# Grouped expert FFN in one kernel: its opening re-ordered (LoRA A and B first, folds, adds and transposes in another order, products in three sweeps)

## What is computed

```
w = weight[adapter_ids];  y = einsum('bsi,boi->bso', x, w)
h = einsum('bsd,nrd->nbsr', y, lora_A);  coef = (2 * lora_weights)[:, None, None]
out = x + einsum('bsd,od->bso', y, W) + bias + einsum('nbsr,nor->bso', h, lora_B * coef)
```

## Time and profile before

| | |
|---|---|
| median of three runs | 1523.1 us |
| profiled execution, its own time | 1520.31 us |
| span in that execution | 1518.6 us |
| PE busy | 1494.0 us, 98% |
| DVE, POOL, ACT busy | 783.4, 460.9, 393.5 us |
| mean granted TensorE clock | 0.996 |

### The profile page before, as it was taken

How to read it: one execution, slowest core, us unless ns; L and a number is a source line. 1 busy time by engine, 2 the same in 40 slices (tenths; PEclk the granted TensorE clock), 3 DMA queues, 4 the chain that set the end, 5 groups by cost and what they waited for, 6 DMA issues and landing times.

```text
span 1518.6 us, 29617 instructions
## 1 busy us (share of the span) xinstructions
PE 1494.0 (98%) x6354; PEld 1192.3 (79%) x6355; DVE 783.4 (52%) x1192; ACT 393.5 (26%) x493; POOL 460.9 (30%) x645
## 2 busy tenths in 40 slices
PE   6989999999999999999999999999999999999998
PEld 3768888888888888888888888888888888888887
DVE  6687666477787277388853333333333433333332
ACT  4244333344444234244431111111111101111010
POOL 4355334433434523525102112112122121221211
PEclk9999999999999999999999999999999999999999
DMA  8988667566787566569835555555455554555554
GB/s 203 327 242 233 162 179 207 164 185 185 201 226 199 167 183 163 178 193 233 211 115 156 144 139 141 136 140 145 132 139 147 140 145 132 141 145 136 141 142 97
DMA packets 172737, 257.90 MB, mean 170 GB/s; under 512 B 31648, under 2 KB 135584, under 8 KB 172704
## 3 DMA queue, kind: packets, MB, share of 16 engines
q1 hardware_dynamic: 130000, 139.14, 35.9%
q10 hardware_dynamic: 22384, 72.76, 16.3%
q0 software_dynamic: 20320, 45.65, 10.4%
HBM read 181.93 MB, written 75.50 MB: 170 GB/s over the span
## 4 chain that ended last, share of the span: by engine, by line
PE 93%; DMA 3%; DVE 2%; SPq 1%; issue 1%; ACT 0%; DVEq 0%; POOL 0%; ACTq 0%; POOLq 0%
PE ps L753 31%; PE ps L755 31%; PE ps L754 31%; DMA x_raw<-in_x_dram 1%; DMA b_raw<-in_L_ffn_lora_B_dram 1%; SPq L207 1%; DMA weff<-fold_sb 1%; DVE w_lo L596 1%; DMA base_sb<-in_L_ffn_W_dram 1%; DVE w_turn L539 0%; SPq L196 0%; SPq L214 0%; DVE fold_sb L655 0%; DVE x_lo L634 0%; DVE x_turn L627 0%
## 5 line engine op out<-in xcount | busy, mean ns | idle before, releaser
L753 PE MATMUL ps<-w_hi,x_hi 128*128 (+1 forms) x2096 | 828.9, 395 | 6.6 <-issue 3.7
L754 PE MATMUL ps<-w_lo,x_hi 128*128 (+1 forms) x2096 | 828.2, 395 | 0.0
L755 PE MATMUL ps<-w_hi,x_lo 128*128 (+1 forms) x2096 | 828.2, 395 | 0.0
L753 PEld LDWEIGHTS ps<-w_hi,x_hi 128*128 128x128 f32 x2096 | 393.5, 188 | 105.8 <-issue 4.8
L755 PEld LDWEIGHTS ps<-w_hi,x_lo 128*128 128x128 f32 x2096 | 393.5, 188 | 96.7
L754 PEld LDWEIGHTS ps<-w_lo,x_hi 128*128 128x128 f32 x2096 | 393.6, 188 | 96.3
L627 DVE STREAM_TRANSPOSE x_turn<-x_raw 128x256 f32<-128x256 f32 x544 | 193.7, 414 | 510.5 <-DMA x_raw<-y_scr 456.0
L207 POOL DMA_DIRECT2D x_raw<-in_x_dram x552 | 294.7, 534 | 399.9 <-DVE x_turn L627 262.2
L421 ACT ACTIVATE x_hi<-x_turn 128x512 fp32r<-128x512 f32 x272 | 167.2, 630 | 697.4 <-DVE x_turn L627 681.0
L396 POOL TENSOR_TENSOR stage<-stage,w_place 128x1024 f32<-128x1024 f32 x64 | 152.8, 2388 | 611.1 <-DMA stage<-in_x_dram 611.1
L634 DVE TENSOR_TENSOR x_lo<-x_turn,x_hi 128x512 fp32r<-128x512 f32 x272 | 180.5, 691 | 133.1 <-ACT x_hi L421 128.4
(11 more groups left out here) (69 smaller groups left out, 38.3 us busy)
## 6 DMA issues: line engine op xcount, KB each, us to landing
w_place<-in_L_cond_weight_dram SPq DMA_DIRECT2D x480, 128.0 KB, 4.2
y_scr<-stage ACTq DMA_DIRECT2D x72, 512.0 KB, 4.1
x_raw<-in_x_dram POOLq DMA_DIRECT2D x552, 64.0 KB, 3.6
x_raw<-y_scr SPq DMA_DIRECT2D x512, 64.0 KB, 2.4
stage<-in_x_dram SPq DMA_DIRECT2D x128, 256.0 KB, 3.7
out_dram<-stage ACTq DMA_DIRECT2D x126, 256.0 KB, 3.0
base_sb<-in_L_ffn_W_dram POOLq DMA_DIRECT2D x8, 512.0 KB, 11.2
weff<-fold_sb POOLq DMA_DIRECT2D x8, 512.0 KB, 11.2
```

The source lines that it names most:

```text
L753: mm(ps[b][:, cols], x_hi[b][:, t, :], hi, start=t == 0, stop=False)
L754: mm(ps[b][:, cols], x_hi[b][:, t, :], lo, start=False, stop=False)
L755: last = mm(ps[b][:, cols], x_lo[b][:, t, :], hi, start=False, stop=t == KT - 1)
```

## The change

The two halved loads of A and B become one load each: A directly behind the ids on SyncE's queue, B first on ScalarE's. Three of the four loads of the first expert's weights (before: two) are issued before the routing tables are there. VectorE transposes only chunk 0, not 0 and 1, before it writes the tables. Five folds instead of six go ahead of slot 0. W gets eight buffers (two of them `stage`) instead of six. VectorE adds six eighths before the x of slot 2 and two behind it, and prepares slot 4's x in the middle of the second expert instead of ahead of it. Slot 4's x is loaded by GpSimd behind the stores of weff instead of by SyncE, and GpSimd's loads for slots 6 and on wait for `w_turned` 14. ScalarE moves slot 0's result only when all adds are done. And `products`, which serves the whole program, runs x_hi w_hi over all eight t, then x_lo w_hi, then x_hi w_lo, each sweep waiting only for its own operands.

```
-    BASES = 6
+    BASES = 8
...
+        base_sb = base_sb[:4] + stage + base_sb[4:]
...
             sp.dma_start(ids_i[:, :], ids.rearrange("(s a) -> s a", a=1)).then_inc(ids_loaded, 16)
-            load_first(sp, 0, (0, 1), w0_loaded)
-            load_b(sp, 0)
-            load_a(sp, 0)
-            load_first(sp, 1, (0, 1), w0_loaded)
+            sp.dma_start(a_sb[:, :], lora_a.rearrange("n r d -> (n r) d")).then_inc(a_loaded, 16)
+            for c in range(LOADS - 1):
+                load_first(sp, c, (0, 1), w0_loaded)
             sp.wait_ge(tables, 1)
             for h in range(2):
                 load_sample(sp, 0, 0, h, first_loaded[0], (0, 1))
-            for c in range(2, LOADS):
-                load_first(sp, c, (0, 1), w0_loaded)
+            load_first(sp, 3, (0, 1), w0_loaded)
...
-            for h in range(2):
-                load_sample(sp, RING, 0, h, first_loaded[0])
...
+            load_first(pool, LOADS - 1, (2, 3), w0_rest)
...
             pool.wait_ge(b_turned, 1)
-            for f in range(4):
+            for f in range(6):
+                load_base(f)
+            pool.wait_ge(w_turned, 6)
+            for f in range(6, FOLDS):
                 load_base(f)
             for h in range(2):
                 load_sample(pool, 3, 3, h, first_rest[3])
-            pool.wait_ge(w_turned, 6)
-            for f in range(4, FOLDS):
-                load_base(f)
             for f in range(FOLDS):
                 pool.wait_ge(base_added, f + 1)
                 pool.dma_start(fold_rows(weff, f), fold_sb[:, f, :]).then_inc(weff_ready, 16)
+            for h in range(2):
+                load_sample(pool, RING, 0, h, first_rest[0])
             load_x(RING + 1, 1)
+
+            pool.wait_ge(w_turned, 2 * CHUNKS - 2)
             load_x(RING + 2, 2)
...
-            load_first(act, 0, (2, 3), w0_loaded)
-            load_b(act, 1)
-            load_a(act, 1)
-            load_first(act, 1, (2, 3), w0_loaded)
+            act.dma_start(b_raw[:, :, :, :].rearrange("p n f r -> p n (f r)"),
+                          lora_b.rearrange("n (p f) r -> p n (f r)", f=FOLDS)).then_inc(b_loaded, 16)
+            for c in range(LOADS - 1):
+                load_first(act, c, (2, 3), w0_loaded)
...
+            act.wait_ge(base_added, FOLDS)
             move_y(0, 0, 0)
             round_x(3, 3)
+
+            act.wait_ge(weff_ready, 16 * FOLDS)
+            round_w(1, 1, range(0, CHUNKS // 2))
             round_x(4, 0)
-
-            act.wait_ge(weff_ready, 16 * FOLDS)
-            round_w(1, 1)
+            round_w(1, 1, range(CHUNKS // 2, CHUNKS))
...
             turn_w(0, 0)
-            turn_w(0, 1)
             dve.wait_ge(listed, 1)
...
             tsc(rank_expert[:, :], ps[2][0:1, 0:EXPERTS + 1], float(EXPERTS), None, ALU.add).then_inc(tables, 1)
+            turn_w(0, 1)
...
+            for f in range(6):
+                add_base(f)
             prepare_first(2)
...
+            for f in range(6, FOLDS):
+                add_base(f)
             prepare_first(3)
+            prepare_w(1, 1, range(0, CHUNKS // 2))
             prepare_first(4)
-            prepare_w(1, 1)
+            prepare_w(1, 1, range(CHUNKS // 2, CHUNKS))
...
-            for f in range(6):
+            for f in range(5):
                 fold(f)
...
+                    pe.wait_ge(w_rounded, ready + (half + 1) * CHUNKS // 2)
+                    for t in range(KT):
+                        if half == 0 and t % (KT // 2) == 0:
+                            pe.wait_ge(x_rounded, n * 2 + (1 + t // (KT // 2)))
+                        mm(ps[b][:, cols], x_hi[b][:, t, :], hi[t], start=t == 0, stop=False)
+                    if half == 0:
+                        pe.wait_ge(x_ready, n * 2 + 2)
+                    for t in range(KT):
+                        mm(ps[b][:, cols], x_lo[b][:, t, :], hi[t], start=False, stop=False)
                     pe.wait_ge(w_ready, ready + (half + 1) * CHUNKS // 2)
-                    cols = slice(half * HALF, (half + 1) * HALF)
                     for t in range(KT):
-                        hi = w_hi[:, bass.ds(par, 1), t, cols].rearrange("p a m -> p (a m)")
-                        lo = w_lo[:, bass.ds(par, 1), t, cols].rearrange("p a m -> p (a m)")
-                        mm(ps[b][:, cols], x_hi[b][:, t, :], hi, start=t == 0, stop=False)
-                        mm(ps[b][:, cols], x_hi[b][:, t, :], lo, start=False, stop=False)
-                        last = mm(ps[b][:, cols], x_lo[b][:, t, :], hi, start=False, stop=t == KT - 1)
+                        last = mm(ps[b][:, cols], x_hi[b][:, t, :], lo[t], start=False, stop=t == KT - 1)
...
             def run_slot(slot, u):
                 used = entry(pe, slot_used, 2 * slot, 1)
-                pe.wait_ge(x_ready, 2 * slot + 2)
                 with pe.If(used > 0):
...
                 with pe.Else():
 
+                    pe.wait_ge(x_ready, 2 * slot + 2)
```

More of the change, by code:

```diff
@@ L161, in grouped_adaln_ffn_kernel @@
         w0_loaded = [sem(f"w0_loaded{c}") for c in range(LOADS)]
-        w0_rest = [sem(f"w0_rest{c}") for c in range(LOADS)]
+        w0_rest = {LOADS - 1: sem("w0_rest")}
         w_loaded = [sem(f"w_loaded{b}") for b in range(RAWS)]
@@ L215, in load_first @@
                               rows[:, :, q * SEG:(q + 1) * SEG]).then_inc(loaded[c], 16)
[L217 to L226, removed]
         @block.sync
@@ L461, in _ @@
             round_x(0, 0)
-            for f in range(3, 6):
+            for f in range(3, 5):
                 move_fold(f)
             round_w(0, 0, [4, 5, 6, 7])
-            for f in range(6, FOLDS):
+            for f in range(5, FOLDS):
                 move_fold(f)
@@ L526, in turn_w @@
                     raw = first_raw[load][:, part * P // BLK:(part + 1) * P // BLK, :]
-                    if part == 0 and load < 2:
+                    if part == 0 and load < LOADS - 1:
                         dve.wait_ge(w0_loaded[load], 16 * QUADS)
@@ L650, in _, with add_base @@
             prepare_first(1)
+            def add_base(f):
+                dve.wait_ge(fold_moved, f + 1)
+                dve.wait_ge(base_loaded[f], 16)
+                tt(fold_sb[:, f, :], fold_sb[:, f, :], base_sb[f][:, :], ALU.add).then_inc(base_added, 1)
+            for f in range(6):
+                add_base(f)
             prepare_first(2)
[L652 to L655, removed]
+            for f in range(6, FOLDS):
+                add_base(f)
             prepare_first(3)
+            prepare_w(1, 1, range(0, CHUNKS // 2))
             prepare_first(4)
-            prepare_w(1, 1)
+            prepare_w(1, 1, range(CHUNKS // 2, CHUNKS))
             for slot in range(1, RING):
@@ L739, in _, with products @@
             pe.wait_ge(b_scaled, 1)
-            pe.wait_ge(a_loaded, 32)
-            for f in range(6):
+            pe.wait_ge(a_loaded, 16)
+            for f in range(5):
                 fold(f)
-            def products(b, par, ready, halves=range(2), end=False):
+            def products(b, par, n, ready, halves=range(2), end=False):
                 for half in halves:
+                    cols = slice(half * HALF, (half + 1) * HALF)
+                    hi = [w_hi[:, bass.ds(par, 1), t, cols].rearrange("p a m -> p (a m)") for t in range(KT)]
+                    lo = [w_lo[:, bass.ds(par, 1), t, cols].rearrange("p a m -> p (a m)") for t in range(KT)]
+                    pe.wait_ge(w_rounded, ready + (half + 1) * CHUNKS // 2)
[7 more added lines that the diff above has]
+                        mm(ps[b][:, cols], x_lo[b][:, t, :], hi[t], start=False, stop=False)
                     pe.wait_ge(w_ready, ready + (half + 1) * CHUNKS // 2)
-                    cols = slice(half * HALF, (half + 1) * HALF)
                     for t in range(KT):
-                        hi = w_hi[:, bass.ds(par, 1), t, cols].rearrange("p a m -> p (a m)")
-                        lo = w_lo[:, bass.ds(par, 1), t, cols].rearrange("p a m -> p (a m)")
-                        mm(ps[b][:, cols], x_hi[b][:, t, :], hi, start=t == 0, stop=False)
-                        mm(ps[b][:, cols], x_hi[b][:, t, :], lo, start=False, stop=False)
-                        last = mm(ps[b][:, cols], x_lo[b][:, t, :], hi, start=False, stop=t == KT - 1)
+                        last = mm(ps[b][:, cols], x_hi[b][:, t, :], lo[t], start=False, stop=t == KT - 1)
                 if halves[-1] == 1:
@@ L759, in products @@
                     last.then_inc(end_half, 1)
-            pe.wait_ge(x_ready, 2)
             pe.wait_ge(fold_moved, 2)
-            products(0, 0, 0, [0])
-            for f in range(6, FOLDS):
+            products(0, 0, 0, 0, [0])
+            for f in range(5, FOLDS):
                 fold(f)
-            products(0, 0, 0, [1])
+            products(0, 0, 0, 0, [1])
             def run_slot(slot, u):
                 used = entry(pe, slot_used, 2 * slot, 1)
-                pe.wait_ge(x_ready, 2 * slot + 2)
```

(14 more changed lines are left out.)

20 lines of the change are left out of this document (8 added, 12 removed).

## The result

The changed kernel took 1511.75 us (median of 6 runs, 1507.98 to 1512.28) against 1521.97 (6 runs beside it): ratio 0.9926, interval 0.9913 to 0.9939, 10.2 us less. The profiled execution took 1507.98 us with a span of 1506.3.

A forecast was written before the change was run, and what follows sets the result against it. PE was taken to be bound, its only idle time around the opening, so E counts: 9.7 us from E, plus 2.0 for a spell gone, minus 1.6 for a new one, gives 10.1 off 1523.1, 1513.0 us; range 1509.0 to 1518.8.

The forecast's parts named there:

- What bounds, and the spacing: PE never waits behind the opening; from 104 us a matmul starts every 233.3 ns, and the sweeps leave that unchanged.
- E: Start of slot 6's products on PE, the later of two chains' ends: 89.5 us forecast, 99.18 before.
- the slower rival: The sweeps widen the matmul spacing, paid 6288 times; 5 ns would cost 31 us, giving 1544; chance 0.04.
- B's landing, 12.0: B, whole at the head of ScalarE's queue, lands at 12.0 us, within bounds 5.0 to 13.0.
- First weights at 15: Chunk 0 of the first weights, behind A and B, reaches VectorE at 15 us; it was 11.24 before.
- PE's own chain, 89.5: Folds, slot 0, slots 1 to 4 and slot 5's dummy on PE end at 89.5 us.
- The charge for a new spell at half clock before slot 0 (1.6): PE's new 1.8 us idleness ahead of slot 0 was charged 1.6 us for running at half clock afterwards.
- weff ready at 62: Second expert's weff: last store issued at 54.4, landing after 7.6 us, so ready at 62 instead of 73.35.
- From weff to slot 6: Second expert's chain from weff to slot 6's rounded x: 23.3 us plus 2.7 for slot 4's x, ending at 88.0.
- the rival's mechanism (second expert last): Second expert late: weff ready only at 67, E 93.0, PE idles 3.5 us, time 1518.5; chance 0.18.
- The spell behind slot 6 goes (2.0): PE's half-clock spell from 99.18 to 103.97 us, after the wait before slot 6, disappears: 2.0 us gained.
- Slot 4's x in the chain behind weff: Preparing slot 4's x inside the second expert adds 2.7 us, but that chain's 88.0 stays under PE's 89.5.

The follow-up runs named there:

- e3_hold_expert: Changed kernel with SyncE waiting for all eight adds before loading chunks 2 and on of the second expert; 1509.17 us.
- e10_x4_hold: Changed kernel with slot 4's x loaded and prepared early, and the second expert's chunks 2 and on held until all adds are done; 1506.21 us.
- e11_x4_six: Changed kernel with slot 4's x loaded and prepared early, and six folds instead of five ahead of slot 0; 1507.68 us.
- e1_halves: Changed kernel with A and B loaded as two halves again, behind load 0 of the weights; 1514.48 us.
- e8_x2_first: Changed kernel with slot 2's x prepared ahead of the six adds again; 1513.81 us.
- e9_six_buffers: Changed kernel with six buffers for W, the seventh and eighth loads waiting for adds behind slot 3's x; 1513.15 us.
- e6_six_folds: Changed kernel with six folds instead of five ahead of slot 0; 1510.72 us.
- after_again: The changed kernel timed and profiled once more, no edit; 1511.36 us.
- e7_x4_early: Changed kernel with slot 4's x loaded by SyncE behind slot 2's and prepared ahead of the second expert; 1507.16 us.
- e2_old_products: Changed kernel with products in their old order, three matmuls per t, waiting for x_lo and w_lo first; 1513.05 us.
- e5_sweeps_alone: Kernel before the change with only the products in three sweeps; 1520.75 us, ratio 0.9996.

## Why the prediction was right, and where its steps failed

The forecast took 10.1 us off the median, and 10.2 were measured. Step by step it was right in some and lucky in others.

- **What bounds, and the spacing**: right. All that changed lies ahead of E; the long stretch has 233.3 to 233.4 ns per matmul in every kernel, so the slower rival fell. Three of the kernels with an early E show 0.6 to 0.7 us of idle time in it (e3_hold_expert, e10_x4_hold, e11_x4_six), so there E is not quite all that counts.
- **B's landing, 12.0**: failed by 5.7 us; it landed at 6.3, near the low bound of 5.0. B and A, 1 MB together, were in at 6.3 and 6.6, both about 4 us after the first data, some 250 GB/s. The forecast had B share the engines from its first piece. In the trace 803 of the 1024 pieces on B's queue had been moved by 4.0 us, against 2 of A's 128, and only from 4.5 to 5.5 us did the queues go one for one, 77 pieces against 79. That second part fits the turn-taking the Trainium skill describes ("DMA: Bandwidth & Descriptors", "Queues, rings and completion order"). The head start, which the forecast lacked, brought B in; why A began so late, issued 0.5 us behind B, is open. The folds started 5.2 us before the 16.4 of the forecast. The forecast also said that an early B would hardly change the sum; e1_halves, with the whole old opening, is 3.1 us slower.
- **First weights at 15**: failed, 11.34. By then 2.6 MB had been moved, not 3, and the rate from 4 to 16 us was 313 GB/s, not 250. Slot 0 started at 23.17 for 27.3, so the title's part is worth more than the 1.0 us of the folds: 2.9 alone, 3.1 inside the change.
- **PE's own chain, 89.5**: it ended at 86.7 (88.95 less the idle 2.24). The charge for a new spell at half clock before slot 0 (1.6) was right for this profile: the next sweep starts 3.40 us after 23.17, where 8 x 0.2333 = 1.87 would do, 1.5 lost. In e8_x2_first, e9_six_buffers and e10_x4_hold that spell is absent.
- **weff ready at 62**: 62.2, by two errors that cancel. The last store was issued at 50.63, not 54.4, and landed after 11.55 us, not 7.6. The count by bytes gave the right number (18 MB at 312 GB/s; the trace has 18.5 MB at 318 from 4 us to 62.2): the DMA engines set this landing, not the last add.
- **From weff to slot 6**: right, 26.0 forecast; the first half of slot 6's x was rounded at 88.1, 25.9 later.
- **E, 89.5**: 88.95 and 90.67 in two profiles, but set by the second expert, which the forecast had 1.5 us under PE's chain. That is the rival's mechanism (second expert last) at the forecast's size, and PE was idle for 2.24 us where the forecast allowed 1. The chain that ended last goes through weff in both profiles, and in e6_six_folds PE's chain made 1.0 us shorter brings nothing.
- **The spell behind slot 6 goes (2.0)**: in one of two profiles. It is there in after_again. This and the later E make the 3.9 us between the two spans; the other runs have no profile.
- **Slot 4's x in the chain behind weff**: counted at 2.7 us, but hidden under PE's chain. It was not hidden; e7_x4_early takes it out, and the time falls by 3 to 4 us.

One slip of arithmetic changes nothing: 11.2 + 2.0 off 1523.1 is 1509.9, not 1509.5.

Taken out of the change one at a time, the whole A and B are worth 3.1 us, the sweeps 1.7, the adds ahead of slot 2's x 2.6 and the two buffers 1.8, while slot 4's new place costs 3 to 4. These overlap and need not add up to 10.2. Not tried one by one: the third early load of weights, the second transpose behind the tables, and the later waits on GpSimd and ScalarE. Not tried at all: a faster way for the ids (4.0 us of wait remain), and fewer bytes ahead of weff.

## What to carry to other kernels

Where a long stretch has no idle time on its engine, forecast one number, the moment it starts, and follow every chain that ends there; the measured gain is the gain of the latest. A row of large stores on full DMA engines lands when all bytes that get their turn before it have been moved, other queues' loads included, so the time at which its last store is issued does not tell it. Work behind a landing goes into the hole that waits for it, not behind it.

## What the runs showed of the hardware beyond expectation

Between the rounding of slot 6's x and the first matmul there is a gap that no shown event explains. The first matmul needs only the first half of x. From the end of that rounding 0.9 us pass in the changed kernel's first profile and 2.2 in its second, and in e7_x4_early, where x was there, 1.1 us pass behind the dummy. The cause is open.

The spell at half clock follows the idle time before slot 6 only roughly. The granted clock from 86 to 110 us was 1.00 behind 0.77 to 2.24 us of idleness and behind 3.24 in e2_old_products. It was 0.93 behind 1.83 in e11_x4_six and behind 3.06 and 3.14, and 0.86 behind 3.03 in e5_sweeps_alone and behind 3.52 and more. e5_sweeps_alone, like the kernel before, also idled ahead of the dummy (2.81 and 2.06 us); the part of that is not separated.

Before slot 0, 2.08 to 2.40 us of idleness had a spell behind it in four profiles, and 2.94 to 3.28 us had none in three (4.68 us in e2_old_products had one). The 20 fold matmuls ahead took 9.59 to 10.02 us in the four and 8.98 to 9.25 in the three. The longest of them lasted 1.22 us in the four and 0.82 to 1.10 in the three, the usual one 0.59. It looks as if the first ones ran at half clock there, but the clock shown as granted is 1.00, so this is not shown. e8_x2_first, of the three:

```profile
23.45 2.10 PE L750 MATMUL ps<-w_hi,x_hi 128*128 128x512 f32 x8 [3.28 <-ACT x_hi L408]
```
